# Attention's hand-overs a block further apart, and a tile's first product repeated up to nine times ahead of the one that counts

## What is computed

```python
xn = _layernorm(x)
# graph: weighted sum of the sources' rows at each destination, then a product with W
gathered = edge_val[:, None] * xn[edge_col]
agg = jax.ops.segment_sum(gathered, edge_row, num_segments=N_NODES)
gnn = jnp.einsum('nd,od->no', agg, W) + b
# attention: q, k = elu(.) + 1; context = k^T v; out = q context / (q k_sum)
D_inv = 1.0 / jnp.maximum(jnp.einsum('bhnd,bhd->bhn', q, k_sum), 1e-06)
context = jnp.einsum('bhnd,bhne->bhde', k, v)
attn = jnp.einsum('bhnd,bhde->bhne', q, context) * D_inv[..., None]
mix = jnp.einsum('bnc,oc->bno', out, Wproj) + bproj
x = x + gnn + mix
x = x + ffn(_layernorm(x))   # top 2 of 8 experts, 256 -> 1024 -> 256
```

## Time and profile before

| what | value |
|---|---|
| median of 3 runs | 2421.96 us (2420.9 to 2422.66) |
| profiled execution | 2401.91 us, its span 2400.1 us |
| mean granted TensorE clock | 0.825 |
| PE busy | 1626.9 us (68%), 13448 matmuls |
| DVE busy | 1423.3 us (59%) |
| ACT busy | 1317.3 us (55%) |
| POOL busy | 1388.1 us (58%) |
| first and last addition of `graph` (L1197) | 332.6 and 1656.9 us |
| gathers of `graph` (L950) | 902, from 324.4 to 1647.3 us |

### The profile page before, as it was taken

The page is one execution under the profiler, slowest core; times in us unless marked ns, Lnnn a source line. Parts: engine busy times, 40 slices in busy tenths (PEclk is TensorE's granted clock), DMA queues, the critical chain, the costliest instruction groups (busy, mean ns, idle before and its releaser), DMA issues. The chain is left out here.

```text
span 2400.1 us, 48331 instructions
## 1 busy us (share of the span) xinstructions
PE 1626.9 (68%) x13448; PEld 1218.7 (51%) x13448; DVE 1423.3 (59%) x3495; ACT 1317.3 (55%) x4250; POOL 1388.1 (58%) x1333
## 2 busy tenths in 40 slices
PE   6877435666666566666564444344549999999998
PEld 3565424454544455455452222222347777777776
DVE  7998535555556565555565555556845555555555
ACT  6455335555555555555555555554556565656555
POOL 3688846666666666666666666665404444444443
PEclk8898868888887788888886565655559999999999
DMA  4022144444444443333333333433512223232222
GB/s 147 14 84 75 58 127 136 133 134 136 136 134 131 130 123 101 104 103 102 104 91 90 93 110 116 154 123 98 173 31 44 50 47 50 45 51 47 48 48 32
DMA packets 139656, 225.26 MB, mean 94 GB/s; under 512 B 33398, under 2 KB 94016, under 8 KB 139298
## 3 DMA queue, kind: packets, MB, share of 16 engines
q0 software_dynamic: 67040, 146.22, 23.5%
q1 hardware_dynamic: 66022, 69.75, 9.2%
q10 hardware_dynamic: 6364, 6.40, 0.8%
HBM read 181.40 MB, written 41.82 MB: 93 GB/s over the span
## 5 line engine op out<-in xcount | busy, mean ns | idle before, releaser
L950 POOL DMA_INDIRECT misc<-z_d,consts x902 | 857.3, 950 | 485.6 <-issue 233.5
L1197 DVE SCALAR_TENSOR_TENSOR acc<-ps,consts,acc 128x256 f32 x902 | 433.7, 481 | 543.9 <-remote 418.9
L975 ACT ACTIVATE misc<-rec,misc 128x128 f16<-128x128 f16 x678 | 230.1, 392 | 275.1 <-DVE rec L1057 202.0
L975 ACT ACTIVATE rec<-rec,misc 128x128 f16<-128x128 f16 x674 | 229.4, 392 | 269.8 <-DVE rec L1057 202.2
L1787 ACT ACTIVATE misc<-ps,misc 128x128 f32<-128x128 f32 x840 | 239.5, 367 | 239.2 <-PE ps L1752 165.4
L1828 POOL DMA_INDIRECT out<-misc,pos x105 | 166.1, 1582 | 291.1 <-ACT misc L1852 258.7
L1752 PE MATMUL ps<-misc,big 128*128 128x128 f16 x1680 | 327.5, 220 | 0.0
L1750 PE MATMUL ps<-misc,big 128*128 128x128 f16 x1680 | 327.2, 220 | 0.2
L1751 PE MATMUL ps<-misc,big 128*128 128x128 f16 x1680 | 327.0, 220 | 0.0
L1767 PE MATMUL ps<-big,rec 128*128 x840 | 319.7, 381 | 0.1
L1279 PE MATMUL ps<-misc 128*128 128x256 f16 x565 | 183.3, 324 | 191.3 <-DVE acc L1197 123.6
(11 more groups left out here) (335 smaller groups left out, 3792.5 us busy)
## 6 DMA issues: line engine op xcount, KB each, us to landing
big<-in_w2T SPq DMA_DIRECT2D x60, 256.0 KB
misc<-z_d,consts POOLq DMA_INDIRECT x902
big<-xT_d SPq DMA_DIRECT2D x98, 128.0 KB
big<-in_w1T SPq DMA_DIRECT2D x32, 256.0 KB
tok_d<-misc SPq DMA_DIRECT2D x50, 132.0 KB, 1.9
xT_d<-misc SPq DMA_DIRECT2D x49, 128.0 KB
z_d<-misc SPq DMA_DIRECT2D x49, 128.0 KB
acc<-in_x SPq DMA_DIRECT2D x1, 6144.0 KB
```

The costliest lines, as they stand in the source:

```text
L950: e.indirect_dma_start(out=rows[k], out_offset=None, in_=c.z_d, in_offset=bass.IndirectOffsetOnAxis(ap=idx[u][:, k:k + 1], axis=0)).then_i ...
L975: e.activation(hot[t % HG][:, half, :], same[t % OG], ACT.Copy, scale=near[n // UG % 3][:, t % UG, 1 + half:2 + half]).then_inc(s_hot, 1)
L1197: e.scalar_tensor_tensor(out=rows_of, in0=out_ps[t % BG], scalar=c.gain, in1=rows_of, op0=ALU.mult, op1=ALU.add).then_inc(s_add[k], 1)
```

## The change

In `rank` the four uses of `fours` become plain Python loops, so the 28 steps are all written out, and `fours` goes. In `graph`:

- V has two PSUM tiles (banks 6 and 7) and its evicted rows three buffers; the normalised row `a` and its turned copy `aT` have two each.
- The context product is made for block s-3, the numerator for b-3, the turn of the result for b-4, the copy of it for b-5 at step 5 (was b-3 at step 4), the projection for b-5, the addition to the accumulator for b-6.
- DVE makes the K and Q features at step 1 (was 3) and the normalised row at step 2 (was 1), for block b-3.
- `fill` says how often a tile's first product is made ahead of the three that count. It goes to the same half bank, which the first counting product overwrites (`start=True`).

The number of turns and the waits of the gathers and additions stay.

```diff
-            fours(e, NG, store)
+            for i in range(NG):
+                store(Turn(i // 4, i % 4, i < NG - 1))
...
-    vo = [matrix(big.take(DH * (P + 1)), DH, P + 1) for _ in range(2)]
+    vo = [matrix(big.take(DH * (P + 1)), DH, P + 1) for _ in range(3)]
...
-    den, a = big.take(NE), big.take(D)
-    aT = matrix(big.take(D), DH, P)
+    den, a = big.take(NE), [big.take(D) for _ in range(2)]
+    aT = [matrix(big.take(D), DH, P) for _ in range(2)]
...
-    v_ps, pj_ps = c.bank[6][:, 0:D], c.bank[7][:, 0:D]
+    v_ps, pj_ps = [c.bank[6 + u][:, 0:D] for u in range(2)], c.bank[7][:, 0:D]
...
                 if k == 4 and live(s - 1):
-                    o = vo[u]
+                    o = vo[(s - 1) % 3]
                     e.wait_ge(s_vz, s)
-                    wait(e, s_ctx, s - 2)
+                    wait(e, s_ctx, s - 3)
...
-                if k == 4 and live(b - 3):
-                    e.wait_ge(s_tr, b - 2)
-                    wait(e, s_pj, b - 3)
-                    e.copy(aT, matrix(tr_ps, DH, P)).then_inc(s_aT, 1)
+                if k == 5 and live(b - 5):
+                    e.wait_ge(s_tr, b - 4)
+                    wait(e, s_pj, b - 6)
+                    e.copy(aT[(b - 5) % 2], matrix(tr_ps, DH, P)).then_inc(s_aT, 1)
...
             def features(h, k, s):
                 u = 1 - h % 2
-                if k == 3 and live(s - 1):
+                if k == 1 and live(s - 1):
                     e.wait_ge(s_ke, s)
...
-                if k == 3 and live(b - 1):
+                if k == 1 and live(b - 1):
                     e.wait_ge(s_qe, b)
...
-                if k == 1 and live(b - 2):
-                    e.wait_ge(s_nd, b - 1)
-                    wait(e, s_tr, b - 2)
+                if k == 2 and live(b - 3):
+                    e.wait_ge(s_nd, b - 2)
+                    wait(e, s_tr, b - 4)
...
-                    if B0 <= at < L0 and x == 0 and live(b - 4):
-                        add_mix(b - 4)
+                    if B0 <= at < L0 and x == 0 and live(b - 6):
+                        add_mix(b - 6)
...
-                if k == 0 and live(s - 2):
-                    e.wait_ge(s_kf, s - 1)
-                    e.wait_ge(s_vo, s - 1)
+                if k == 0 and live(s - 3):
+                    e.wait_ge(s_kf, s - 2)
+                    e.wait_ge(s_vo, s - 2)
...
                 if k == 3 and live(s):
-                    wait(e, s_vo, s)
+                    wait(e, s_vo, s - 1)
...
-                if k == 0 and live(b - 2):
+                if k == 0 and live(b - 3):
...
-                    e.wait_ge(s_qf, b - 1)
-                    wait(e, s_at, b - 2)
+                    e.wait_ge(s_qf, b - 2)
+                    wait(e, s_at, b - 3)
...
-                if k == 3 and live(b - 2):
-                    e.wait_ge(s_at, b - 1)
-                    wait(e, s_aT, b - 2)
+                if k == 3 and live(b - 4):
+                    e.wait_ge(s_at, b - 3)
+                    wait(e, s_aT, b - 4)
...
-                if k == 5 and live(b - 3):
-                    e.wait_ge(s_aT, b - 2)
-                    wait(e, s_mix, b - 3)
+                if k == 5 and live(b - 5):
+                    e.wait_ge(s_aT, b - 4)
+                    wait(e, s_mix, b - 5)
...
+            def fill(at, t):
+
+                if at < B0:
+                    return (0, 0, 4, 0, 4, 4)[t % 6]
+                return (0, 0, 3, 2, 3, 0)[t % 6] if at < L0 else 9
+
             def product(j, t):
...
                 o, w = out_ps[t % BG], hot[t % HG]
+                for _ in range(fill(j, t)):
+                    e.matmul(o, w[:, 0, :], rows[k][:, 0:D], start=True, stop=True)
                 e.matmul(o, w[:, 0, :], rows[k][:, 0:D], start=True, stop=False)
```

More of the change, by code:

```diff
@@ L154, in next @@
         return Turn(self.j + self.u // 3, (self.u + 1) % 4)
[L157 to L167, removed]
 def rank(nc, c, A):
@@ L525, in _ @@
             column(Turn(0, 0))
-            fours(e, NG, hot)
+            for i in range(NG):
+                hot(Turn(i // 4, i % 4, i < NG - 1))
         @block.scalar
@@ L607, in sorting @@
                 evict(s)
-            fours(e, NG, sorting)
+            for i in range(NG):
+                sorting(Turn(i // 4, i % 4, i < NG - 1))
         @block.tensor
@@ L828, in graph @@
     M2, M9, LAST = 8, 16, 25
-    assert 4 * B0 >= NT + 3 and 4 * (L0 - B0) >= NT + 5 and L1 + 5 <= LOOPS and 24 * L1 >= 3 * CW // 2
+    assert 4 * B0 >= NT + 3 and 4 * (L0 - B0) >= NT + 6 and L1 + 5 <= LOOPS and 24 * L1 >= 3 * CW // 2
     out_ps = [c.bank[k // 2][:, k % 2 * D:k % 2 * D + D] for k in range(BG)]
@@ L993, in features @@
                             e.copy(o[:, m, P:P + 1], c.valid).then_inc(s_vend, 1)
-                        e.activation(o[:, :, 0:P], matrix(v_ps, DH, P), ACT.Copy, scale=c.valid).then_inc(s_vo, 1)
+                        e.activation(o[:, :, 0:P], matrix(v_ps[u], DH, P), ACT.Copy, scale=c.valid).then_inc(s_vo, 1)
                     else:
-                        e.copy(o[:, :, 0:P], matrix(v_ps, DH, P)).then_inc(s_vo, 1)
+                        e.copy(o[:, :, 0:P], matrix(v_ps[u], DH, P)).then_inc(s_vo, 1)
             def attention(h, k, b):
@@ L1047, in turn @@
                     weigh(j, t)
-            e.wait_ge(s_ones, 4)
+            e.wait_ge(s_ones, 5)
             fetch(0)
@@ L1061, in _ @@
             v = Chain(e, s_v)
-            for z in (ones, vo[0], vo[1]):
+            for z in (ones, vo[0], vo[1], vo[2]):
                 e.memset(z, 1.0).then_inc(s_ones, 1)
@@ L1224, in features @@
                 if k == 3 and live(s):
-                    wait(e, s_vo, s)
+                    wait(e, s_vo, s - 1)
+                    if s == 1:
+                        e.wait_ge(s_bias, 2)
                     for x in range(DH):
-                        l = e.matmul(v_ps, xT[h][:, x, :], wv[:, x, :], start=x == 0, stop=x == 1)
+                        l = e.matmul(v_ps[s % 2], xT[h][:, x, :], wv[:, x, :], start=x == 0, stop=x == 1)
                     l.then_inc(s_vz, 1)
             def attention(j, h, k, b):
-                if k == 0 and live(b - 2):
-                    if isinstance(b, int) and b == 2:
+                if k == 0 and live(b - 3):
+                    if b == 3:
                         e.wait_ge(s_bd, 1)
-                    e.wait_ge(s_qf, b - 1)
-                    wait(e, s_at, b - 2)
+                    e.wait_ge(s_qf, b - 2)
+                    wait(e, s_at, b - 3)
                     for m in range(DH):
-                        l = e.matmul(nd_ps[:, m, :], qf[h % 2][:, m, :], sums[:, m, :], start=True, stop=True)
+                        l = e.matmul(nd_ps[:, m, :], qf[(b - 3) % 2][:, m, :], sums[:, m, :], start=True, stop=True)
                     l.then_inc(s_nd, 1)
```

14 lines of the change are left out of this document (7 added, 7 removed).

## The result

The changed kernel takes 2454.48 us (median of 4 runs, 2454.27 to 2455.97) against 2421.44 us for the kernel before, measured with it: a ratio of 1.0137 with an interval of 1.0124 to 1.0149. It is 33 us slower, where 99 us faster were forecast. The profiled execution took 2454.27 us (span 2452.5). The one of before was 20 us under its median, so the two profiles differ by 52 us where the medians differ by 33.

What follows compares the result with a forecast made beforehand. The prediction took GpSimd's gathers, 1.25 us a tile, as the floor, with 197 us excess from late news of TensorE's products. Terms -21 - 38 - 40 = -99 us took 2422 to 2323 us, range 2240 to 2480.

Steps and rivals of the forecast that it cites:

- What bounds the kernel: Three aggregation stages: GpSimd's gathers set a floor of 1.25 us a tile; 197 us excess comes from late news of TensorE.
- What the products do to the stalls: Features and attention: repeated products remove half the excess of 75 and 80 us, -38 and -40 us.
- last stage at 1.33 us a tile: Last 254 tiles: with nine repeats TensorE replaces GpSimd as the bound at full clock, 338 us, -21 us.
- common cause: Aggregation stalls: late news and low clock both come from TensorE's swing between dense and empty; no separate size.
- rival B: Aggregation: only products get faster, stalls have their own cause; loosened waits give 0 to 27 us, 2405 us; chance 0.11.
- Rival D: Last stage: stalls stay and repeats take away the catching up, +120 us, 2542, or 2606 with features; chance 0.26.
- milder form: Last stage: a weaker rival D in which half the stall stays, +40 to +60 us; half of D's 0.26.
- Hand-overs at 0 to -27: Features and attention: looser waits for the K feature and normalised row, alone worth 0 to -27 us.
- Unrolled sort at 0: Sort: only register and branch work goes while GpSimd paces it, 0 us, bounds -5 and +5.
- Repeats in features and attention hidden by the gathers: Features and attention: TensorE needs 6.8 and 6.4 us a block at full clock, under the 7.5 us of six gathers.
- The rule against the change: Last stage: if a low clock only slows products, idle time over 200 us hides it and more products cannot pay.

Runs made afterwards that it cites:

- e4: Kernel before with gathers for the first 12 tiles only, whose rows all later tiles use again; 1927.9 us in one run.
- e1: Changed kernel without repeated products, hand-overs and unrolled sort kept, on a chip with prompt news; 2206.6 us, ratio 0.9980 to the kernel before.
- e3: Kernel before with only the sort's loops written out, on a chip with prompt news; 2207.8 us, ratio 0.9991 to the kernel before.
- e9: Kernel before with the repeats of features and attention and none in the last stage; ratio 1.0006, last stage 321.5 us.
- e11: Kernel before with each last-stage count of finished products given three tiles later, no repeats; last stage 319.7 us.
- e12: Kernel before with each last-stage count given three tiles later and nine repeats a tile there; last stage 385.7 us.
- e5: Changed kernel itself, unaltered, on a chip with prompt news; 2220.7 us, ratio 1.0044 to the kernel before, last stage 331.7 us.
- e6: Kernel before, unaltered, profiled on a chip with prompt news; 2210.7 us, last stage 321.9 us.

## Why the prediction was wrong

**What bounds the kernel: right.** GpSimd's 1.25 us a tile is the floor; every stage holds it where news is prompt, and e4 shows that only the gathers set it. The excess was rightly put down to late counts of finished products, too: on the other chips they come within 0.1 us and the excess is gone.

**The step that failed is "What the products do to the stalls", -38 and -40 us**, and with it the last stage at 1.33 us a tile (-21 us), which supposed no stalls at all. By the profiles the three came to +16.6, +7.8 and +28.4 us. It rested on one sentence, that late news and the swing of the clock have a common cause. The swing was taken away (clock 1.00, PE busy 90% of the last stage) and the news stayed 2 to 5 us late; on the other chips the clock is low (0.52) and the news is prompt. Neither half of "they go together" survives. The evidence against it stood in the prediction itself, as rival B's: the count of 1380.98 is late while the clock is at 0.98. The experts, which I set against B and D, share neither the gathers' pace nor the waits of those stages. There news is prompt on the first chip with TensorE 99% busy; in the changed last stage, with TensorE 90% busy, it is not.

**The last stage's price: right as a product, wrong as a time on this chip.** (3 + 9) x 0.109 = 1.31 us gives 333 us; measured 331.2 to 331.7 where news is prompt. On the first chip it is 387.5, the same work and 57 us of pauses of TensorE, a term that the prediction did not have. Rival D, slower because the repeats take away the catching up, had the direction and the place: before, TensorE was idle for over 200 us and could wait; after, it is the bound and whatever stops it is paid. But its sum, of stalls that stay and longer bursts (+120), is not what the trace shows, and the +33 of the medians lies under its milder form (+40 to +60), the +52 of the profiles in it, so that its nearness is partly luck. Its condition, that late signals don't care how busy PE is, holds by half: they stay late, but 1 of 251 is over 5 us late where it was 103 of 182. Pauses inside the repeats were in none of the rivals.

**Hand-overs at 0 to -27: right where news is prompt, not tested alone where it is late.** Alone with prompt news they bring 1.2 us beyond the unrolled sort (2207.8 to 2206.6), and the intervals of e1 and e3 overlap. On the first chip the waits did move: PE's wait for the K feature (122.8 us) is gone (the context product has 11.0 us of "issue" ahead of it), and 44.5 us for the addition stand in its place; in attention 129.1 us for L1101 became 80.1 for the same row at the numerator. I had not said what is late next, though the change leaves the numerator one PSUM tile.

**Unrolled sort at 0: right**, the start of the aggregation stays at 332.5 us. **Repeats in features and attention hidden by the gathers: right** where news is prompt (e9, ratio 1.0006).

**The rule against the change.** The Trainium skill (TensorE: Matmul & The Clock Gate, "Terms") prices a throttled clock as slower products only. The runs agree in the direct sense: with six repeats the clock rises from 0.52 to 0.99 and the stage becomes 3 us longer. By that rule the time should have been rival B's; the rule was right about the clock and has nothing on the price of holding it up.

**Open.** What makes TensorE's counts late and TensorE pause on the first chip: it is not the code alone (the kernel is the same), not a low clock, and not a TensorE that falls empty; no run came back to that chip. So the part of the 33 us beyond the 9 of prompt news is located, for the last stage, and not explained. Open too are the features' 16.6 us and attention's 7.8, and how far repeats or moved hand-overs take part in them: within the repeats there the pauses over 0.25 us add only 1.9 and 3.4 us.

## What to carry to other kernels

A low clock on an engine that wasn't the bound cost nothing here, and dummy products that hold it up are work: price them against the bound (here 0.04 us a tile too much), and ask what the engine's idle time was good for. An engine with idle time waits for free; filled up with dummy products it pays each wait and each pause in full (e11 against e12). When a profile names the releaser of a wait, check it by the order of time: in e12 it named ScalarE where the addition ended the wait. And a time that agrees is no proof of a mechanism: compare where in the program the delays stand. Before a stall is explained from within a kernel, run it on a second chip; 210 of 2421 us would have been known not to be the kernel's.

## What the runs showed of the hardware

- The same kernel took 2421 us on one chip and 2209 to 2212 on four others (medians; single executions from 2207 to 2220); the record does not name the first one. The difference lies in the three stages of the aggregation, where counts of finished products came up to 12 us late; in the experts of the changed kernel's execution 389 of 396 came within 0.1 us.
- On that chip the lateness differs with the load: 103 of 182 counts over 5 us late with TensorE 43% busy, 1 of 251 with TensorE 90% busy, but then 218 of them by 2 to 5 us. VectorE's counts in the same stages (294 and 378) all came within 0.1 us.
- There TensorE also paused between products that wait for nothing: 125 steps over 0.125 us, 56.7 us in all, in 387.5 us of the changed kernel's last stage; in e5, the same code, two steps and 0.6 us.
- A gather of 128 rows holds GpSimd for 0.95 us and the next starts 0.30 us after its end (e6, all gathers of the last stage; 237 of these waits are put down to nothing else): 1.25 us is the floor.
- Twelve products of 128x128 by 128x256 in float16 took 1.304 us a tile at the full clock over 254 tiles, 0.109 each, and seventeen 1.846.
